# Looked-up rows ahead of gathered rows in the first layer of a graph network on TensorE

## The reference

```python
h = jnp.maximum(_layernorm(x, axis=-1), 0.0)
e_feat = jnp.concatenate([h[src], h[dst], edge_attr], axis=-1)   # 400000 x 96
hid = jax.nn.relu(e_feat @ W1 + b1)                              # 64 wide
v = hid @ W2 + b2                                                # 32 wide
x_cand = jax.ops.segment_max(v, dst, num_segments=12500)
out = x + jnp.maximum(x_cand, h)
```

## Time and profile before

| what | value |
|---|---|
| median of 3 runs | 4759.54 us (4758.01 to 4763.21) |
| span of the profiled execution, first to last instruction | 3219.5 us |
| PE busy | 3007.4 us, 93% |
| POOL busy | 2408.5 us, 75% |
| mean granted clock of PE | 0.970 of full |

### The profile page before, as it was taken

One profiled execution on the slowest core, in us unless ns is written; L12 is line 12 of the kernel. 1 busy time (PEld: TensorE's weight loads), 2 busy tenths in 40 slices (PEclk: granted clock), 3 DMA queues, 4 the chain that ended last, 5 costly groups with the idle time before them and its releaser, 6 DMA issues. The chain is left out here.

```text
span 3219.5 us, 56263 instructions
## 1 busy us (share of the span) xinstructions
PE 3007.4 (93%) x19600; PEld 2221.8 (69%) x19600; DVE 2189.0 (68%) x2420; ACT 2124.3 (66%) x2489; POOL 2408.5 (75%) x2547
## 2 busy tenths in 40 slices
PE   7999999999999999999999999999998998999910
PEld 5776677777777777777777777777776775777700
DVE  6321677777777777777777777777775775777743
ACT  4335677777777777777777777777775775777710
POOL 6777777777777777777777777777777777777756
PEclk9999999999999999999999999999999998999965
DMA  8940333333333333333333333333333333333321
GB/s 270 359 172 27 85 101 101 101 100 98 96 97 98 100 99 100 100 102 100 88 99 98 100 97 101 100 98 80 112 98 85 100 82 95 95 97 98 86 51 26
DMA packets 194362, 337.82 MB, mean 105 GB/s; under 512 B 74114, under 2 KB 118100, under 8 KB 193711
## 3 DMA queue, kind: packets, MB, share of 16 engines
q1 hardware_dynamic: 112264, 291.52, 26.6%
q0 software_dynamic: 81216, 41.73, 10.2%
q10 hardware_dynamic: 738, 3.21, 0.3%
HBM read 227.85 MB, written 108.41 MB: 104 GB/s over the span
## 5 line engine op out<-in xcount | busy, mean ns | idle before, releaser
L558 POOL DMA_INDIRECT src_in<-h_dram,src_ix x2293 | 2167.0, 945 | 698.8 <-issue 637.8
L794 PE MATMUL ps_rows<-onehot,table 128*128 128x512 f32 x9800 | 2290.4, 393 | 28.0 <-DVE onehot L1054 28.0
L794 PEld LDWEIGHTS ps_rows<-onehot,table 128*128 128x128 f32 x9800 | 1832.3, 189 | 501.8 <-issue 107.2
L719 ACT ACTIVATE onehot<-distance 128x1024 fp32r<-128x1024 bf16 x882 | 878.8, 1049 | 696.8 <-PE ps_rows L794 696.8
L714 ACT ACTIVATE distance<-picks,below_column 128x1024 bf16<-128x1024 int16 x882 | 954.8, 1136 | 49.3 <-DMA picks<-picks_dram 49.3
L1054 DVE SCALAR_TENSOR_TENSOR onehot<-picks,column,ps_layers 128x1024 fp32r<-128x1024 int16 x392 | 493.0, 1278 | 356.2 <-PE ps_rows L794 340.6
L1104 DVE STREAM_TRANSPOSE ps_layers<-rows_in 128x512 f32<-128x512 f32 x196 | 129.5, 706 | 236.6 <-ACT hid L705 198.3
L1108 DVE TENSOR_TENSOR_SCAN dst_t<-mask_in,dst_t,ps_layers 128x512 f32<-128x512 bf16 x196 | 251.0, 1280 | 7.0
L705 ACT ACTIVATE hid<-ps_layers,b_col 128x512 f32<-128x512 f32 x392 | 234.0, 674 | 28.1 <-PE ps_layers L824 28.1
L1121 DVE TENSOR_TENSOR_SCAN max_t<-mask_in,max_t,ps_layers 128x512 f32<-128x512 bf16 x192 | 245.4, 1278 | 3.5
L1125 DVE STREAM_TRANSPOSE rows_in<-max_t 128x512 f32<-128x512 f32 x196 | 210.8, 1115 | 3.4
(11 more groups left out here) (112 smaller groups left out, 1102.3 us busy)
## 6 DMA issues: line engine op xcount, KB each, us to landing
picks<-picks_dram SPq DMA_DIRECT2D x98, 512.0 KB
first_rows<-hid SPq DMA_DIRECT2D x100, 500.0 KB, 4.1
rows_in<-in_edge_attr_dram SPq DMA_DIRECT2D x97, 512.0 KB
rows_in<-first_rows SPq DMA_DIRECT2D x97, 512.0 KB
run_max<-rows_in SPq DMA_DIRECT2D x96, 512.0 KB
src_in<-h_dram,src_ix POOLq DMA_INDIRECT x2293
mask_in<-mask_dram SPq DMA_DIRECT2D x97, 256.0 KB
h_dram<-h_sb ACTq DMA_DIRECT2D x1, 1568.0 KB
```

What stands on the lines that cost most here:

```text
L558: pool.indirect_dma_start(out=src_in[:, slot, g, r, :], out_offset=None, in_=rows[:, :], in_offset=bass.IndirectOffsetOnAxis(ap=src_ix[:, ...
L719: nc.scalar.activation(onehot[:, RING_AT[c] + BY_DVE[c] + k, :, :].rearrange("p g w -> p (g w)"), distance[:, k, :], ACT.Relu, bias=1.0, s ...
L794: mm = nc.tensor.matmul(ps_rows[g][side][:, 0:WIDE], table[:, i * SIDES + side, part, :], onehot[:, RING_AT[c] + t, g, :], start=(i + part ...
```

## The change

Within `layer_one` the looked-up group is put ahead of the gathered group, with its wait for `rows_masked`; the wait for `src_turned` goes behind it. The gathered matmuls are now the ones with `stop=True`, and those of g = 1 count up `hid_summed`. The number of instructions of each kind is the same.

```diff
-                pe.wait_ge(src_turned, j * 2 + 2)
                 gathered = [GATHERED, LAST_GATHERED if last else GATHERED]
-                for g in range(2):
-                    for a in range(A):
-                        nc.tensor.matmul(ps_hid[a][g * HID:(g + 1) * HID, 0:gathered[g]], w_src[chunk(a), :], src_t[chunk(a), g, 0:gathered[g]],
-                                         start=False, stop=False)
                 pe.wait_ge(rows_masked, j * MASKS + MASKS)
                 for a in range(A):
                     for g in range(2):
-                        mm = nc.tensor.matmul(ps_hid[a][g * HID:(g + 1) * HID, gathered[g]:gathered[g] + PICKED], w_src[:, :],
-                                              picked_rows[:, slot, g, a * PICKED:(a + 1) * PICKED], start=False, stop=True)
-                    mm.then_inc(hid_summed, 1)
+                        nc.tensor.matmul(ps_hid[a][g * HID:(g + 1) * HID, gathered[g]:gathered[g] + PICKED], w_src[:, :],
+                                         picked_rows[:, slot, g, a * PICKED:(a + 1) * PICKED], start=False, stop=False)
+                pe.wait_ge(src_turned, j * 2 + 2)
+                for g in range(2):
+                    for a in range(A):
+                        mm = nc.tensor.matmul(ps_hid[a][g * HID:(g + 1) * HID, 0:gathered[g]], w_src[chunk(a), :], src_t[chunk(a), g, 0:gathered[g]],
+                                              start=False, stop=True)
+                        if g:
+                            mm.then_inc(hid_summed, 1)
```

## The result

The changed kernel takes 4773.96 us (median of 8 runs, 4762.47 to 4792.17), the kernel before 4757.32 beside it (8 runs). The ratio is 1.0041, 95% interval [1.0027, 1.0055]: +19.5 us, between +13 and +26. That is over the 0.2% that a measurement can tell, so the change made the kernel slower by 0.4%. (The ratio is taken over the runs; the two medians alone lie 16.6 us apart.) The time lies in the predicted range, but only because the range was drawn out to the first rival, 4778, which had a chance of 0.12; what was forecast with 0.85, no measurable change, did not come.

The account below looks back on a forecast made before the run. POOL's gathers, 30.0 us a pair against PE's 27.73, were taken as the slower part, hiding most of 0.185 us a pair; the end's +2.5 us on 4759.54 gave 4762.0 us, range 4752 to 4779.

Parts of the forecast that it names:

- the first rival: In the loop, PE sets the pace in the timed runs: 18.6 us slower, 4778 us; chance 0.12.
- Sum: Whole kernel: span 3219.5 plus 2.5 gives 3222.0; the unexplained 1540 us up to the median kept, so 4762.0 us.
- What bounds the kernel: In the loop, PE looks like the bound at 27.73 us a pair, but POOL's 24 gathers take 30.0 and never wait.
- What hides it: Pairs 75, 76 and 82: PE's 34.0 us of held time absorbs the cost; only 2.6 us after pair 83 stays.
- pair 75's 28 to 29 us: Sign in the loop: pair 75 falls from 42.06 us to about 28 to 29 as its waiting for POOL shrinks.
- pair 83 at 2700.4: Sign in the loop: pair 83 begins within 1 us of 2700.4, as before the change.
- The price per pair: On PE in layer_one, one more entry and exit of 32-row tiles costs 0.05 + 0.135 = 0.185 us a pair.
- bound, -0.10 or 0.37: Lower and upper limits in us a pair on PE, from the looked-up-into-gathered contact costing nothing or all of it twice.
- the rival of a free re-ordering: On PE in layer_one, the new order costs nothing or gains; the end gives -0.6 us, 4759 us; chance 0.17.
- The signals: hid_summed in layer_one comes about 0.4 us later, fits into DVE's 1.09 us wait for PE and costs nothing.
- The end: Pairs 96 and 97: relus of 96 come 3.86 us after layer_one, +0.8; with pair 97's paths, +2.5 us in all.
- The gathers' path: In pair 97, gathered matmuls start when src_turned allows, at 3074.68, so relus begin at 3075.4, 0.6 us earlier.

Follow-up runs that it names:

- before_again: The kernel before, without an edit, profiled again; 4761.93 us, ratio 1.0006 to the kernel before.
- after: The changed kernel: looked-up group ahead of the gathered group in layer_one, against the kernel before; 4773.96 us, ratio 1.0041.
- after_again: The changed kernel, without an edit, profiled again; 4787.2 us, ratio 1.0048 to the kernel before.
- after_by_chunk: The changed kernel, but gathered matmuls go chunk by chunk, each chunk's sum signalled as it finishes; 4786.61 us, ratio 1.0053 to the kernel before.
- signals_last: The kernel before with its group order, but looked-up matmuls go by g then a and all four sums are signalled at the end; 4772.07 us, ratio 1.0028.
- split_picked: The kernel before, with looked-up chunks 0 and 1 moved ahead of the destination group, 2 and 3 staying last; 4862.0 us, ratio 1.003.
- held_after: The changed kernel, gathers in two bursts with a pause, layer_one released by a memset behind the last gather; 4556.13 us, ratio 0.9361 to the kernel before.
- paced_before: The kernel before, a pair's 24 gathers issued in one go behind hid_summed, next layer_one waiting for a semaphore increment placed after them; 5177.5 us, ratio 1.0675.
- bursts_before: The kernel before, gathers in bursts of ten and fourteen with a wait for eight tiles between, layer_one waiting for a semaphore increment; 4579.71 us, ratio 0.9625.

## Why the prediction was right or wrong, point by point

**The frame (wrong).** The first step that failed is in "Sum": the 1540 us "are shown by no row; I keep them as they are". A constant outside the span would leave the loop as the profile shows it; it is 91 pairs that take 43.4 instead of 27.7 us and a longer prelude. The trace alone couldn't say so, but the prediction's "against" on the first rival (the clock is 0.970) used the clock of the very execution that was in doubt. In the timed kind the clock is 0.82.

**What bounds the kernel (wrong).** "POOL is slower. ... it never waits for PE" held for the execution shown. In the timed kind POOL waits 353 times for PE. A pair is its 24 gathers, 30.0 us, and further idle time, ended nearly always by PE's tiles or DVE's `src_turned`, of 13.4 us in before_again and in after and 13.7 in after_again. "What hides it", the second step that failed, fell with it: no hold at L516, so no 34.0 us at pairs 75, 76 and 82 to hide in. There was nothing to compare with pair 75's 28 to 29 us, or with pair 83 at 2700.4.

**The price per pair (right).** 0.185 predicted; 27.73 to 27.91 in the five clean pairs, +0.16 over all pairs without the gathers. The two contacts that had no row, looked-up into gathered and gathered into look-up, cost what their neighbours did: neither bound, -0.10 or 0.37, came near. This also ends the rival of a free re-ordering on PE at full pace. The Trainium skill's rule in the prediction, which by its three changes gave 0.135, was as near to 0.16 as 0.185 was for the kernels without gathers; the clean pairs of after speak for 0.18. That a change of tiling mode costs time the trace bears out.

**The first rival (came true, by another road).** It gave 96 x 0.185 + 0.8 = 18.6 us; measured were +19.5, +22.8 and, without gathers, +21.1. That the price adds up to the loss is shown only without the gathers. In the full kernels it agrees in size, which may in part be luck. The rival named a lower clock as the condition. That is half right: the clock is lower, 0.82, but without the gathers, and so without the gaps, it is 0.955. And its condition "PE sets the pace" is loose: PE is held by nothing that the profile names, while POOL gathers, and POOL then waits for PE's tiles.

One place where the orders differ in the full kernels is the contact behind the last group: from the last matmul start of layer_one to the first of the look-up it is 0.71 us in before_again (mean of the 91 long pairs) and 0.91 in after, 0.89 in after_again, 0.92 in after_by_chunk, but 0.69 in signals_last and 0.72 in split_picked. POOL's gathers end 14.6 us after layer_one starts in before_again and 14.5 in after, ahead of this contact, so no gap of layer_one stands behind it that could hide the 0.2; 91 x 0.2 is 18 us. But it isn't purely the price of tile heights: the last matmul has 384 columns instead of 128, and in the clean pairs the same contact is 0.20 and 0.41. Both orders have another 0.5 us there in the long pairs. The kernels whose last group is the gathered one lose about their whole clean price (0.18: +19.5, +22.8, +25), those that end with looked-up rows only a part (0.50: +13; 0.33: +14.5). That fits prices inside the gaps being partly covered; it wasn't tried apart.

**The signals (right).** A shift of 0.4 us was to cost nothing. Counted from the first look-up matmul, the relus came 0.43 us later in after and 0.12 in after_again than in before_again, and after_by_chunk, whose signals come first of all, is no faster.

**The end (wrong in its path, near in its sum).** Pair 96, 96's relus and layer_two, and pair 97 in after:

```profile
4609.16 1.11 PE L809 MATMUL ps_layers<-ea_t,w_edge 32*64 32x512 f32 x16
...
4613.11 2.42 ACT L705 ACTIVATE hid<-ps_layers,b_col 128x512 f32<-128x512 f32 x4 [11.80 <-PE ps_layers L824]
4615.63 1.96 PE L837 MATMUL ps_rows<-hid,w_out 64*32 64x512 f32 x16 [2.64 <-issue]
4617.52 1.57 PE L809 MATMUL ps_layers<-ea_t,w_edge 32*64 32x512 f32 x16
```

The relus follow layer_one by 3.95 us (predicted 3.86; 3.09 before, 3.10 in before_again). Layer_one of 97 comes 8.36 us after that of 96, and in before_again 4613.16 - 4606.20 = 6.96: +1.4 instead of +0.8, because layer_two starts after a longer pause and runs wholly at the lower level, 1.89 us, where before_again has 1.34. Pair 97's own relus follow at 4.40 us in both. The gathers' path in the prediction, which at the end let PE wait for rows of pair 97, doesn't exist in timed executions: the last gather is issued at 4438.44, 179 us before layer_one of 97. So +1.4 us, with +2.5 predicted.

**What stays open.** Four things. Why the first profiled execution had no gaps. How gathering takes the work away from PE: the gaps have no releaser, the larger of the two instruction queues moved the same in the execution without gaps as in after (121 packets, 0.99 MB and 0.1% for q14), and no row shows when an instruction reached PE. The Trainium skill, "Runtime: NRT & Kernel Launch", section "Instruction fetch mechanics", says that an engine fetches its instructions ahead and that this is mostly hidden. If the gaps are late instructions, this case's trace disagrees, with layer_one at 16.35 us beside gathers and 3.57 without; that they are is my reading, not shown. Whether it is the issuing of the gathers or their own traffic that PE suffers from: the edit took both away. And whether the loss in the full kernels is the clean price, since two versions lose less than theirs and held_after loses nothing that can be measured.

## What to carry to other kernels

Before a prediction rests on a profile, set its span against the timed median: 3219.5 against 4759.54 us meant that the profile was of something else, and no term from it on who waits for whom could be trusted, while prices of clean groups (0.18 us for two changes of tile height) still could. Where matmuls beside a GpSimd that issues indirect DMAs come singly with idle time that nothing releases, try to move the DMA issues before touching the order on PE: two bursts with a pause, and the dense stretch released from behind the last gather, gave 6.5%; one burst without a pause cost 6.8%; the order of groups was worth 0.4%. When a release must come after DMAs are issued, let it be counted by an instruction of the engine itself, and look in the timeline whether it does.

## What the runs showed of the hardware

- While POOL issues indirect DMAs, 1.25 us each, PE gets gaps that nothing in the profile releases: float32 passes come singly or few at a time, up to 3.1 us apart, whatever matmul it is (128 or 512 columns), and at full pace again 2 to 5 us after the start of POOL's last gather. The gaps began 14 us after POOL went on in paced_before and 5 us in before_again. On one chip 4757 us with the gathers; on another 4846 with and 3358 without. One execution of the same program, 3219.5 us long, had none of these gaps beside the same gathers.
- A semaphore increment placed behind indirect DMAs in POOL's program came 10.1 us (bursts_before) and 14.0 us (paced_before) ahead of the last one's issue; a memset's came behind it, and PE started 0.6 us after the memset.
- In the looked-up group (128 by 64 tiles, 128 columns) the order g, a takes 1.51 us where a, g takes 1.02, for the same 8 matmuls.
